# A graph attention layer on one core: inputs transposed by the host, queries projected once in three bf16 parts, gathers from resident indices with eight slots

## The reference

```python
Q = (x @ WQ).reshape(N, H, dh)
K = (x @ WK).reshape(N, H, dh)
V = (x @ WV).reshape(N, H, dh)
Eh = (edge_attr @ WE).reshape(-1, H, dh)
src, dst = (edge_index[0], edge_index[1])
score = K[src] * Q[dst] / jnp.sqrt(jnp.float32(dh)) * Eh
score = jnp.exp(jnp.clip(score.sum(-1, keepdims=True), -5.0, 5.0))
msg = V[src] * score
wV = jax.ops.segment_sum(msg, dst, num_segments=N)
Z = jax.ops.segment_sum(score, dst, num_segments=N)
h_attn = (wV / (Z + ATTN_EPS)).reshape(N, D)
h = x + h_attn
mean = h.mean(axis=0)
var = jnp.mean((h - mean) ** 2, axis=0)
return (h - mean) * jax.lax.rsqrt(var + BN_EPS) * bn_gamma + bn_beta
# the layer returns layernorm(x + the value above), over the features
```

## Time and profile before

| | us |
|---|---|
| plain runs, median (lowest, highest) | 2381.82 (2377.86, 2384.34) |
| profiled execution, span | 3072.1 |
| first gather starts, in the profile | 105.31 |
| last sum of the edge stage ends | 2958.6 |
| 1664 gathers, busy | 1656.1 |
| VectorE busy, ScalarE busy | 1610.1, 976.2 |

### The profile page before, as it was taken

How to read it: one execution, slowest core, us unless ns; L and a number is a source line. 1 busy time by engine, 2 the same in 40 slices (tenths; PEclk the granted TensorE clock), 3 DMA queues, 4 the chain that set the end, 5 groups by cost and what they waited for, 6 DMA issues and landing times.

```text
span 3072.1 us, 60981 instructions
## 1 busy us (share of the span) xinstructions
PE 2715.4 (88%) x18106; PEld 2290.2 (75%) x18106; DVE 1610.1 (52%) x3767; ACT 976.2 (32%) x3157; POOL 1747.8 (57%) x1747
## 2 busy tenths in 40 slices
PE   6788998999899989889899899989899889898995
PEld 5677777777777777777777777777777777787773
DVE  4455455455455545555555545555555455555558
ACT  4323233232233322332232223322333233222346
POOL 3455565555565555555555555555555565655545
PEclk8678688787777877887787877877887788778765
DMA  6444343333343433343433433443333444434312
GB/s 230 132 116 117 113 116 117 116 118 111 109 117 116 117 110 112 115 118 114 116 118 112 115 116 113 116 117 114 114 118 113 117 118 113 121 112 118 112 33 83
DMA packets 152900, 355.04 MB, mean 116 GB/s; under 512 B 35671, under 2 KB 36183, under 8 KB 152885
## 3 DMA queue, kind: packets, MB, share of 16 engines
q0 software_dynamic: 79872, 218.21, 24.4%
q1 hardware_dynamic: 73013, 136.65, 14.9%
HBM read 335.52 MB, written 19.20 MB: 115 GB/s over the span
## 4 chain that ended last, share of the span: by engine, by line
PE 82%; issue 9%; another core or an unknown queue 3%; DVE 2%; DMA 1%; ACT 1%; SPq 1%; ACTq 0%; DVEq 0%; POOL 0%; POOLq 0%
PE qe_ps L737 18%; PE eh_ps L746 18%; PE agg_ps L756 15%; PE eaT_ps L723 10%; PE agg_ps L758 9%; PE ohT_ps L726 6%; PE qw_ps L728 4%; PE qe_ps L829 1%; DMA ea<-in_x 1%; PE eh_ps L685 1%; DVE onehot L1116 1%; SPq L334 0%; PE qe_ps L685 0%; PE eaT_ps L820 0%
## 5 line engine op out<-in xcount | busy, mean ns | idle before, releaser
L448 POOL DMA_INDIRECT kv<-kv_rows,idx x1664 | 1656.1, 995 | 1202.7 <-ACT idx L552 748.0
L961 DVE TENSOR_TENSOR kq<-kv,qe_ps 128x512 f32<-128x512 f32 x416 | 285.0, 685 | 792.1 <-remote 531.4
L737 PE MATMUL qe_ps<-qwin,node_room 64*128 64x128 f32 x3328 | 612.0, 336 | 27.0 <-issue 26.9
L746 PE MATMUL eh_ps<-we_sb,eaT 128*128 128x128 f32 x3328 | 620.9, 343 | 6.1 <-issue 5.7
L737 PEld LDWEIGHTS qe_ps<-qwin,node_room 64*128 64x128 f32 x3328 | 515.8, 233 | 132.7 <-issue 128.3
L746 PEld LDWEIGHTS eh_ps<-we_sb,eaT 128*128 128x128 f32 x3328 | 524.6, 240 | 73.4 <-issue 39.4
L552 ACT CAST idx<-src_t 128x4 int32 (+1 forms) x416 | 80.3, 193 | 1532.8 <-PE agg_ps L758 991.2
L756 PE MATMUL agg_ps<-onehot,kv 128*128 128x64 f32 x3328 | 545.3, 321 | 23.0 <-DVE kv L951 13.8
L756 PEld LDWEIGHTS agg_ps<-onehot,kv 128*128 128x128 f32 x3328 | 534.8, 244 | 30.1 <-issue 29.3
L723 PE MATMUL eaT_ps<-ident,ea 128*128 128x128 f32 x1664 | 342.2, 325 | 122.6 <-issue 109.7
L967 DVE TENSOR_TENSOR kq<-kq,eh_ps 128x512 f32<-128x512 f32 x416 | 286.1, 688 | 251.9 <-PE eh_ps L746 118.3
(11 more groups left out here) (103 smaller groups left out, 1554.3 us busy)
## 6 DMA issues: line engine op xcount, KB each, us to landing
ea<-in_edge_attr SPq DMA_DIRECT2D x416, 256.0 KB
kv<-kv_rows,idx POOLq DMA_INDIRECT x1664
kv_rows<-kv SPq DMA_DIRECT2D x24, 512.0 KB, 3.7
ea<-in_x SPq DMA_DIRECT2D x24, 256.0 KB, 4.2
out<-kv SPq DMA_DIRECT2D x24, 256.0 KB, 2.0
acc<-in_dst SPq DMA_DIRECT2D x1, 624.0 KB
acc<-in_src SPq DMA_DIRECT2D x1, 624.0 KB
kv_rows<-kv SPq DMA_DIRECT2D x1, 212.0 KB
```

The lines of the kernel that those rows point to most:

```text
L448: pool.indirect_dma_start(out=kv[:, s, j, :], out_offset=None, in_=kv_rows, in_offset=bass.IndirectOffsetOnAxis(ap=idx[:, s, j:j + 1], axi ...
L737: last = pe.matmul(qe_ps[s % 2][:, j * P:(j + 1) * P], ohT[:, s % 2, j * P:(j + 1) * P], qwin[:, s % 2, :], start=True, stop=True)
L746: last = pe.matmul(eh_ps[s % 2][:, j * P:(j + 1) * P], eaT[:, s % 2, j * P:(j + 1) * P], we_sb[:, :], start=True, stop=True)
L961: nc.vector.tensor_tensor(kq[:, :, :], kv[:, s, :, 0:D], qe, ALU.mult).then_inc(kq_done, 1)
```

## The change

**Host.** x is given transposed (xT, padded to 12672 nodes), edge_attr transposed in groups of [128 features, 512 edges] (padded to 416 x 512), `src` and `dst` as tables of [128, 1664], the first destination of each group as a list.

**Prologue.** xT is loaded in eight pieces into the room of `z_sum`; TensorE multiplies without transposes (L514); ScalarE and VectorE each copy half a chunk and the rows are stored as before. After all of them have been multiplied, all queries are projected once (L527). ScalarE takes the bf16 part of a chunk, VectorE the rest (L686), ScalarE that rest's bf16 part, VectorE what still remains (L688): three bf16 parts whose sum is the float32 value. They are stored as `q_rows`, three rows of 128 bf16 for each node. Table and stray flag are made after that, in a [128, 1664] pass each (L692, L695); the gathers start behind the flag.

**Edges.** The window is 42 nodes; three parts make 126 rows, which SyncE loads for each group as `q_win`. ScalarE writes the float32 one-hot (168 columns) three times over as bf16 (504 columns); TensorE turns it and spreads the queries with four bf16 matmuls of 126 rows. No transposes of edges and no projection of a window are left. The scores are summed by four matmuls, each tile into its own strip of partitions (0, 32, 64, 96) of `z_ps`, and `z_sum` keeps four strips. There are eight slots for rows, edges and windows; the loop has eight groups a turn (50 looped turns, the first and last written out). GpSimd's 1664 gathers are written out and take their indices from the resident table; they wait for the sums of the group eight before and for nothing else.

**Epilogue.** TensorE's turn of z is four matmuls of 104 partitions with a constant that adds the four strips (L619), ScalarE's step is a small one (L586 and after), xT is loaded again into the room of the ring. All steps are written out.

```diff
-WIN = 64
-UNROLL = 4
+WIN = 42
+PARTS = 3
+ROWS = WIN * PARTS
+SLOTS = 8
...
-                    pool.wait_ge(idx_ready, n + 1)
-                    pool.sem_inc(gather_begun, 1)
+                if n >= SLOTS:
+                    pool.wait_ge(agg_ready, n - SLOTS + 1)
...
-                            in_offset=bass.IndirectOffsetOnAxis(ap=idx[:, s, j:j + 1], axis=0),
+                        in_offset=bass.IndirectOffsetOnAxis(ap=src_t[:, n * TILES + j:n * TILES + j + 1], axis=0),
...
-            with pool.Fori(0, TURNS) as i:
-                gathers(i)
+            for n in range(NG):
+                gather(n)
...
+                nc.scalar.copy(q_st[:, s, 0:j, 0, :], q_ps[s][:, 0:j * P].rearrange("p (j d) -> p j d", j=j)).then_inc(q_hi, 1)
+                nc.scalar.copy(z_sum[:, c * NB:c * NB + j * P], zero_col[:, :].to_broadcast([P, j * P])).then_inc(z_clear, 1)
+                act.wait_ge(q_rem, c + 1)
+                nc.scalar.copy(q_st[:, s, 0:j, 1, :], q_rest[:, b, 0:j, :]).then_inc(q_mid, 1)
...
+            for s in range(SLOTS):
+                dve.wait_ge(kv_stored[s], 16 * len(range(s, CHUNKS, SLOTS)))
+            for c in range(CHUNKS):
+                s, b, j = c % 4, c % 2, tiles_of(c)
+                dve.wait_ge(q_hi, c + 1)
...
+                nc.vector.tensor_tensor(q_rest[:, b, 0:j, :], whole, q_st[:, s, 0:j, 0, :], ALU.subtract).then_inc(q_rem, 1)
+                dve.wait_ge(q_mid, c + 1)
+                nc.vector.tensor_tensor(q_st[:, s, 0:j, 2, :], q_rest[:, b, 0:j, :], q_st[:, s, 0:j, 1, :], ALU.subtract).then_inc(q_lo, 1)
...
+                thrice = onehot[:, s % 4].unsqueeze(3).to_broadcast([P, TILES, WIN, PARTS])
+                nc.scalar.copy(onehot_b[:, s % 4].rearrange("p j (w k) -> p j w k", k=PARTS), thrice).then_inc(onehot_cast, 1)
...
-                    last = pe.transpose(eaT_ps[:, j * P:(j + 1) * P], ea[:, s, j, :], ident[:, :])
-                last.then_inc(eaT_ready, 1)
...
-                pe.matmul(qw_ps[0:WIN, 0:D], xw[:, s % 2, :], w_q[:, :], start=True, stop=True).then_inc(qw_ready, 1)
...
-                    last = pe.matmul(qe_ps[s % 2][:, j * P:(j + 1) * P], ohT[:, s % 2, j * P:(j + 1) * P], qwin[:, s % 2, :], start=True, stop=True)
+                    last = pe.matmul(qe_ps[s % 2][:, j * P:(j + 1) * P], ohT[:, s % 2, j * P:(j + 1) * P], q_win[:, s, :], start=True, stop=True)
...
-                    last = pe.matmul(agg_ps[0:HEADS, WIN:2 * WIN], score[:, j * HEADS:(j + 1) * HEADS], onehot[:, s, j, :], start=(j == 0), stop=(j == TILES - 1))
+                    last = pe.matmul(z_ps[32 * j:32 * j + HEADS, 0:WIN], score[:, s % 2, j * HEADS:(j + 1) * HEADS], onehot[:, s % 4, j, :], start=True, stop=True)
...
+                    nodes = z_sum[0:3 * 32 + HEADS, k * HC + j * HQ:k * HC + (j + 1) * HQ]
+                    last = pe.matmul(zT_ps[b][0:HQ, j * HEADS:(j + 1) * HEADS], nodes, gather8[0:3 * 32 + HEADS, :], start=True, stop=True)
```

1238 lines of the change are left out of this document (536 added, 702 removed).

## The result

The changed kernel takes 2413.97 us (median; 2408.66 to 2416.78) beside 2381.27 us for the old one measured with it: a ratio of 1.0131 with the interval 1.0112 to 1.0150. It is slower, by 33 us or 1.3%, where the forecast was slower by 13. A second measurement gave 2411.86 against 2382.09, ratio 1.0129 (1.0113 to 1.0146).

The account below looks back on a forecast made before the run. The plain kernel was taken as paced by the issue of gathers, with TensorE close behind. Prologue 128 + loop 2134 + tail 9 + epilogue 124 = 2395 us, 0.55% above the median; range 2275 to 2470.

Parts of the forecast that it names:

- rival 2: Edge loop: 1.25 us a gather is the profiled execution's only, TensorE paced the old kernel; 1842 to 2299 us, chance 0.18.
- rival 4: Edge loop: halts at the loop's branch, at most 0.7 us a turn, get hidden; pace 5.00 to 5.05, chance 0.05.
- Rival 3: Edge loop: TensorE's clock could stay at the half, 5.95 us a group; 2736 us, or 2480 if partial; chance 0.08.
- The step on collisions: Edge loop: VectorE's weighting or one-hot lengthens gathers starting beside it; 0.13 us a group taken, 5.13 x 416 = 2134 us.
- TensorE's saving: Edge loop: at the full clock 1.5 us a group saved lie beside the gathers and are worth nothing.
- the slots: Edge loop: lifting the limit of four slots takes away waits, in plain runs no more than 0.18 us a group.
- First gather 128: Prologue: stores at 64, queries 55, then table, flag and branch; first gather at 128 us, 23 later, bounds 118 and 142.
- The chain of the queries' parts: Prologue: 25 chunks through VectorE, ScalarE, VectorE at 2.25 us each, 49 to 64 us, taken 55.
- the hand-over of 0.1 us: Prologue, query projection: three hand-overs a chunk at 0.1 us each, taken between nothing and 0.17.
- Table, flag and branch: Prologue: two table passes of 2.25 us each, 4.5, then sum, flag and branch 3.6 and 0.9 ahead of them.
- The lower bound of the text, 118: Prologue: earliest start forecast for the first gather, 118 us, against the expected 128.
- the +10: Epilogue, attention stage: z turned by matmuls, 1.95 to 2.77 us a step, +20 at half clock; half taken, giving 124 us.

Follow-up runs that it names:

- ctl_before: The old kernel with no edit, profiled beside its own plain runs: 2382.41 us, ratio 1.0011.
- b_psum2: The old kernel with the scores for VectorE's weighting read from PSUM: 2321.03 us, ratio 0.9750 to the old kernel.
- a_psum2: The changed kernel with the scores for VectorE's weighting read from PSUM: 2377.32 us, ratio 0.9983 to the old kernel.
- the first series: First set of follow-up runs, edited variants of the changed and old kernels, beside an old kernel that took 3121.82 us there.
- a_four: The changed kernel with gathers waiting for the sums of the group four before instead of eight: 2411.37 us, ratio 1.0125 to the old kernel.
- a_spread: The changed kernel with ScalarE's spread of step k put before its shift of step k+1 in the attention stage: 2385.90 us, ratio 1.0022 to the old kernel.
- a_strip: The changed kernel with four tiles' scores summed in one strip of eight partitions and z turned by transposes: 2389.19 us, ratio 1.0032 to the old kernel.
- ctl_after: The changed kernel with no edit, measured a second time: 2411.86 us beside 2382.09 for the old kernel, ratio 1.0129.
- a_yshift: The changed kernel with VectorE's small layer-norm shift moved ahead of normalising chunk c+3: 2395.52 us, ratio 1.0060 to the old kernel.
- b_light: The old kernel without three of the four matmuls that sum a group's scores: 3515.30 us, ratio 1.128 to the old kernel at 3121.82.
- a_early: The changed kernel with table, stray flag and GpSimd's branch ahead of the query projection: 2823.24 us, ratio 0.905 to the old kernel at 3121.82.
- a_psum: The changed kernel with the scores for VectorE's weighting read from PSUM: 2828.63 us, ratio 0.907 to the old kernel at 3121.82.

## Why the prediction was right and wrong

**What paces the kernel: right.** The forecast set the profile's "TensorE 88%" aside and read 5.18 us a group as GpSimd's 5.00 and some stretch. ctl_before has 5.177 in its profile, b_psum2 and a_psum2 take the stretch away. The *reason* that rival 2 gave for the 690 us between profile and plain runs was wrong: in ctl_before the profile has the plain time. By its likeness to the first series the 690 us belong to another condition, in which plain runs take 3100 us as well, and in that profile 82% of the chain is TensorE's. Rival 2, built on a distortion, fell with it, and so did rival 4: the old kernel's halts are no part of its 2381 us. Rival 3's condition came true and its price did not: TensorE's granted clock in the loop fell from 1.00 in ctl_before to 0.69, and no gather waited for it. That holds at 2381 us for the old kernel; at 3122 even the variants of the changed kernel were not paced by gathers.

**The loop: right in kind, 18 us too high.** Forecast 5.13 a group and 2134 us; measured 5.087 and 2116.3. The gain was put at 20 us and is 37. The step on collisions named the cause, and both operations that it named stretch gathers, the weighting nine parts in ten (31.4 and 3.5 us). What it could not say is how often they meet: the weighting's share was 24.9 to 37.8 us in the profiles of the changed kernel, a_four, a_spread, a_strip and ctl_after, whose loops differ little. That the 0.13 us a group was near the 0.087 measured is in part luck. TensorE's saving was put at nothing, and it is nothing, as is that of the slots (a_four).

**The prologue: 15 us too high.** First gather 128, measured 112.8. Three terms were too high. The stores were done at 58.8 instead of 64. The chain of the queries' parts took 1.98 us a chunk instead of 2.25, 48.8 in all instead of 55: the hand-over of 0.1 us was a middle between nothing and 0.17, and two were 0.03 to 0.04 and the third was hidden, since the next rest starts before the recorded end of the low part. Table, flag and branch took 5.3 instead of 9; the first pass over the table took 1.02 us instead of 2.25. The lower bound of the text, 118, was still above what came.

**The epilogue: 43 us too low, and this is where the forecast missed.** It said 113.7 + 10 = 124 from the last sum to the end and got 167.0, +53. The term was worked out from TensorE's instructions alone, 1.95 to 2.77 us a step. With ScalarE's order mended (a_spread) the step takes 2.41, +11.5 us, close to the +10, but by luck: the +10 was half of the 20 that the text worked out for the half clock, taken in case the stage ran at the full one. The clock was 0.50, and the turn took 1.70 us and overlapped the turn back by 0.36. Two waits were not in the term. (1) ScalarE's list: the old first step read z_sum, the new one waits for TensorE's turn, and the spread is queued behind it. What is queued behind a waiting instruction was worked out for the gathers and not here; it costs 1.06 us x 25 = 26. (2) The clash of VectorE's shift with GpSimd's addition in the layer norm, 17 us, which the diff hides: the two operations stand where they stood, but the start of the shift fell behind GpSimd's start by 0.14 us. In the old kernel's profile, VectorE and GpSimd:

```profile
3029.24 0.68 DVE L1111 TENSOR_SCALAR eaT<-acc,bn 128x512 f32 x1
...
3030.12 0.12 DVE L1132 SCALAR_TENSOR_TENSOR ymr<-ymv,yrec 128x4 f32<-128x4 f32 x1
...
3030.16 1.26 POOL L483 TENSOR_TENSOR ea<-eaT,xT 128x512 f32<-128x512 f32 x1 [0.54 <-DVE eaT L1111]
```

The shift starts 0.04 us ahead of the addition. The addition follows the normalising (L1111) by 0.24 us here and by 0.08 in the changed kernel (L869 ends at 2348.70, L384 starts at 2348.78), and the normalising is 0.17 shorter there. In ctl_before the hand-over is 0.08 in the first, third and fourth chunks and in the last, which GpSimd's list has written out, and 0.17 to 0.28 in the looped ones between. The change writes all of them out, which by these rows lets GpSimd's addition start ahead of the shift. It was not tried alone, nor is it shown what shortens the normalising.

**The sum.** 112.8 + 2116.3 + 177.7 = 2406.8, against 128 + 2134 + 133 = 2395: errors of -15, -18 and +45 leave +12. The span was close because two terms were too high and one too low. The time lay inside the range (2275 to 2470) and the sign was right, but the difference to the old kernel, +13, was less than half of the 33 that came. The step that failed is the epilogue's +10: it left out ScalarE's spread queued behind a wait for TensorE, 26 us by a_spread, and the blocked shift, 16 us by a_yshift.

## What to carry to other kernels

Where the busiest engine of a profile doesn't fit the plain time, compute each engine's bare price a turn and see which one does, and take a profile beside plain runs that give the time in question. When an operation is given a new input, look at what is queued behind it on its own engine, in the small stages as well: one swapped pair of lines was worth 26 us here, nearly as much as the 32 us of hiding the query stage. Look, too, at how a changed or written-out loop moves the starts of operations on two engines against each other: a shift by 0.2 us made a clash here where there was none. And keep VectorE's operations with two operands in SBUF out of the way of GpSimd's, or put one operand into PSUM.

## What the runs showed of the hardware

- An indirect DMA of 128 rows of 1 KB costs GpSimd 0.945 us and 0.30 to the next, whatever the other engines do in these loops, except that a VectorE operation with both operands in SBUF (the weighting, 128x512, or the one-hot, 128x168 and 128x256) that runs when it starts holds it to 0.82 us behind that operation's end. With one of the weighting's operands in PSUM 35 instead of 171 gathers are long, all 35 beside the one-hot.
- GpSimd's addition of 512 columns holds a VectorE operation on four columns with two operands in SBUF that starts 0.14 us behind it to its end, 1.15 us instead of 0.12. One that starts 0.03 us behind it is not held (five chunks of ctl_before, 0.12 us each).
- With three of a group's four score-sum matmuls left out, TensorE had a lower clock (0.82 to 0.88 instead of 0.965) in three of four runs, and the old kernel took 150 to 270 us longer (b_light2); what lowered it is open.
- The old kernel took about 2382 us in four series (granted clock 0.965 in ctl_before) and 3122 at 0.775 in one, and chip number 2 saw both. In the second condition TensorE was busy without a gap at the half clock in b_light (7.96 us a group), and in the changed kernel's variants TensorE's signal of finished sums came about 2.5 us late (a_early, a_psum). What sets this condition is open.
